# Six local-attention layers: probabilities in blocks of 32 queries by 64 keys, and another order of work on all engines

## The reference, cut to what matters

```python
def local_attention(q, k, v):
    b, h, n, d = q.shape            # 8, 16 heads, 512 tokens, 64
    w = WINDOW                      # 32
    ...
    bk2, bv2 = (look(bk), look(bv)) # each window of 32 with the one before it
    ...
    mask = (it < jb) | (it > jb + w) | (jb == -1)
    sim = jnp.einsum('bhwie,bhwje->bhwij', bq, bk2) * QK_SCALE
    sim = jnp.where(mask, -jnp.finfo(sim.dtype).max, sim)
    attn = jax.nn.softmax(sim, -1)
    out = jnp.einsum('bhwij,bhwje->bhwie', attn, bv2)
    return out.reshape(b, h, n, d)
```

## Time and profile before

| what | value |
|---|---|
| three runs | 3644.83, 3644.83, 3644.84 us (median 3644.83) |
| span of the profiled execution, first to last instruction | 3639.9 us |
| PE busy | 3554.4 us (98%), 47348 matmul instructions |
| PE weight loads busy | 3028.6 us (83%) |
| ACT busy | 3359.9 us (92%) |
| DVE busy | 3128.2 us (86%) |
| POOL busy | 2732.9 us (75%) |
| granted TensorE clock | 1.000 over the span |

### The profile page before, as it was taken

The page is one execution under the profiler, slowest core; times in us unless marked ns, Lnnn a source line. Parts: engine busy times, 40 slices in busy tenths (PEclk is TensorE's granted clock), DMA queues, the critical chain, the costliest instruction groups (busy, mean ns, idle before and its releaser), DMA issues.

```text
span 3639.9 us, 133048 instructions
## 1 busy us (share of the span) xinstructions
PE 3554.4 (98%) x47348; PEld 3028.6 (83%) x47348; DVE 3128.2 (86%) x7021; ACT 3359.9 (92%) x10928; POOL 2732.9 (75%) x2058
## 2 busy tenths in 40 slices
PE   8999999999999999999999999999999999999998
PEld 5666678888888888888888888888888888888887
DVE  8999988888888788887888888889888888888887
ACT  8999889999999999999999999999999999999996
POOL 0111288888888788788888888888888888888884
PEclk9999999999999999999999999999999999999999
DMA  2000011111111111111111111111111111111111
GB/s 102 7 14 10 14 38 43 35 32 34 44 43 41 28 36 36 39 46 36 33 33 40 40 45 35 33 30 43 47 35 37 30 33 45 34 35 36 42 36 39
DMA packets 165015, 132.71 MB, mean 36 GB/s; under 512 B 113933, under 2 KB 124813, under 8 KB 164109
## 3 DMA queue, kind: packets, MB, share of 16 engines
q1 hardware_dynamic: 164365, 124.19, 13.9%
HBM read 25.84 MB, written 4.19 MB: 8 GB/s over the span
## 4 chain that ended last, share of the span: by engine, by line
PE 75%; ACT 5%; DVE 4%; issue 3%; POOL 1%; ACTq 0%; POOLq 0%; DVEq 0%
PE bank L1103 10%; PE bank L1057 10%; PE bank L1082 8%; PE bank L1143 8%; PE bank L1125 6%; PE bank L1019 4%; PE bank L1020 4%; PE bank L1021 4%; PE bank L980 4%; PE bank L1118 3%; PE bank L953 2%; ACT late L1441 2%; PE bank L955 2%; PE bank L954 2%; PE bank L1033 2%
## 5 line engine op out<-in xcount | busy, mean ns | idle before, releaser
L1554 POOL TENSOR_TENSOR a_rn<-a_ssqc,a_minus_half 128x16 f32<-128x16 f32 x384 | 1113.2, 2899 | 490.3 <-DVE a_ssqc L1765 480.6
L1441 ACT ACTIVATE late<-bank,a_negmax 128x96 f32<-128x96 f32 x3072 | 1013.5, 363 | 11.8 <-DVE a_negmax L1714 10.7
L1577 POOL TENSOR_TENSOR a_r<-a_u,a_rn 128x512 f32<-128x512 f32 x768 | 788.3, 1046 | 0.6
L1564 POOL TENSOR_TENSOR a_PN<-late,a_erec 128x384 f32<-128x384 f32 x768 | 730.6, 971 | 9.1 <-PE bank L1082 8.2
L1441 ACT ACTIVATION_READ_ACCUMULATOR late<-bank,a_negmax 128x1 f32 x3072 | 708.7, 231 | 0.0
L1424 ACT ACTIVATE a_QK<-bank 128x512 f32<-128x512 f32 x768 | 467.8, 609 | 122.5 <-PE bank L1057 122.5
L1737 DVE TENSOR_TENSOR a_v<-bank,a_rot_s 128x512 f32<-128x512 f32 x768 | 523.1, 681 | 0.0
L1727 DVE TENSOR_TENSOR a_u<-bank,a_rot_c 128x512 f32<-128x512 f32 x768 | 521.4, 679 | 1.2 <-ACT a_sq L1417 1.1
L1417 ACT ACTIVATE a_sq<-bank 128x512 f32<-128x512 f32 x768 | 482.7, 628 | 42.2 <-PE bank L1021 12.9
L1402 ACT ACTIVATE late<-bank 128x512 f32<-128x512 f32 x758 | 479.6, 633 | 15.3 <-PE bank L1082 11.4
L1745 DVE TENSOR_TENSOR a_u<-a_u,a_v 128x1024 f32<-128x1024 f32 x384 | 489.5, 1275 | 0.7 <-issue 0.3
(11 more groups left out here) (191 smaller groups left out, 8129.7 us busy)
## 6 DMA issues: line engine op xcount, KB each, us to landing
a_V_even<-a_V_odd SPq DMA_DIRECT2D x384, 128.0 KB, 2.3
a_V_even<-a_V_odd SPq DMA_DIRECT2D x192, 64.0 KB, 2.2
late<-in_qkv SPq DMA_DIRECT2D x20, 384.0 KB, 3.8
a_x_sh<-X SPq DMA_DIRECT2D x48, 128.0 KB
a_V_even<-a_V_odd SPq DMA_DIRECT2D x192, 32.0 KB, 1.9
a_x_sh<-X SPq DMA_DIRECT2D x48, 127.0 KB
late<-X SPq DMA_DIRECT2D x47, 128.0 KB
late<-X SPq DMA_DIRECT2D x47, 127.0 KB
```

The source lines that it names most:

```text
L1441: ins = act.activation(E[:, s.par, k, :], scores[:, i % 2, col:col + KW], ACT.Exp, bias=negmax[:, s.par, k:k + 1], accum_out=esum[:, s.par ...
L1554: pool.tensor_tensor(rn[:, a.par, :], ssqc[:, a.par, :], minus_half[:, :], ALU.pow).then_inc(S["rn"], 1)
L1564: pool.tensor_tensor(PN[:, s.par, 2 * hp:2 * hp + 2, :].rearrange("p i (b k) -> p i b k", b=2)[:, :, :, 0:KW], spread(E[:, s.par, half, :] ...
L1577: pool.tensor_tensor(heads(r[:, a.par, half]), heads(u[:, a.par, half]), rn[:, a.par, mm * 2 * HG:(mm + 1) * 2 * HG].unsqueeze(2).to_broad ...
```

## The change

The block becomes 32 queries by 64 keys (KW = 2 * WIN). The scores of a pair are 8 x 64 columns on 128 partitions: the query windows c = 0 to 3 lie on partitions 32c to 32c + 31, head e in score bank e. PE's logits become 32 matmuls of 64 rows, 32 output partitions and 64 columns; its mask becomes 8 matmuls of 256 columns; the transposes of the probabilities become one set of four 128x128; the outputs become 32 matmuls of 64 rows, 64 output partitions and 32 columns, which write two banks (5 and 6), one for each half of the key partitions. ACT copies the transposed probabilities once, not twice, and the outputs from both banks in one instruction. The values are moved by DMA into V_sh, by 32 partitions, 96 rows and 32 rows in place of 64 and 32. The LAG constants and the order on PE, ACT, DVE and POOL change: on PE it becomes outputs, projections, values, then mask and logits, transposes of the probabilities, transposes of queries and keys 1, output projection, transposes of queries and keys 0. The norms, the second cosines and sines, the sum, and the power move one cycle later. The core of the diff (in the cycles of PE, ACT and DVE "..." stands for the lines taken out, which are in the kernel above):

```diff
-KW = 3 * WIN
+KW = 2 * WIN
...
-LAG_T, LAG_S, LAG_PT, LAG_O, LAG_Y = 2, 4, 6, 7, 7
+LAG_R, LAG_T0, LAG_T1, LAG_Q0, LAG_Q1, LAG_L, LAG_S, LAG_PT, LAG_O, LAG_Y = 1, 1, 2, 2, 3, 4, 5, 6, 7, 7
...
-    sb("masks", [P, 2, 2 * KW], BF16)
+    sb("masks", [P, 2, 4 * KW], BF16)
...
-    A["PT"] = view("layers", 16 * P, "p (s n q) -> p s n q", s=2, n=8)
-    A["OT"] = view("layers", 4 * CQ, "p (s e t) -> p s e t", s=2, e=2)
+    A["PT"] = view("layers", 16 * P)[:, 0:8 * P].rearrange("p (s n q) -> p s n q", s=2, n=4)
+    A["OT"] = view("layers", 4 * CQ, "p (s u h t) -> p s u h t", s=2, u=4, h=2)
...
-    sb("PN", [P, 2, 4, 2 * P])
+    sb("PN", [P, 2, 4, P])
...
-    p_qk, p_vo, p_ta, p_tb, p_y = banks[0:2], banks[2], banks[5], banks[6], banks[7]
+    p_qk, p_ta, p_vo, p_tb, p_y = banks[0:2], banks[2], banks[5], banks[6], banks[7]
+    p_o, p_both = (p_vo, p_tb), psum[:, 5:7, 0:CQ]
...
-                sp.dma_start(V_even[WIN:KW, a.g, m:m + 2, :], V_odd[0:64, a.g, m:m + 2, :]).then_inc(S[name], 16)
+                sp.dma_start(V_sh[WIN:P, a.g, m:m + 2, :], V_nat[0:P - WIN, a.g, m:m + 2, :]).then_inc(S[name], 16)
...
-                t = pair_at(n, p, LAG_T)
+                t = pair_at(n, p, LAG_T1 if mm else LAG_T0)
...
-                    ge(pe, S[f"pt_out{mm}"], done(n, p - (mm == 0), LAG_PT))
+                    if mm == 0:
+                        ge(pe, S["pt_out"], done(n, p, LAG_PT))
+                    else:
+                        ge(pe, S["o_out"], done(n, p, LAG_O))
...
-            def transpose_probs(n, p, hp):
...
-            def prob_transposes(t, hp):
-                for i in range(4):
-                    first = KW if i % 2 else 0
-                    ins = pe.transpose(p_t[hp][:, i * P:(i + 1) * P], PN[:, t.par, 2 * hp + i // 2, first:first + P], ident[:, :])
-                ins.then_inc(S[f"pt{hp}"], 1)
+                    for e in range(2):
+                        pe.wait_ge(S[f"pn{e}"], t.k + 1)
+                    pe.wait_ge(S["qk_out0"], done(n, p - 1, LAG_T0))
...
+            def prob_transposes(t):
+                for k in range(4):
+                    ins = pe.transpose(p_ta[:, k * P:(k + 1) * P], PN[:, t.par, k, :], ident[:, :])
+                ins.then_inc(S["pt"], 1)
...
+                    pe.wait_ge(S["qk_out1"], keys_out)
...
-                        for i in range(4):
-                            keys = slice(0, P if i % 2 else KW)
-                            V = (V_odd if i % 2 else V_even)[keys, o.g, 2 * o.half + i // 2, :]
-                            for e in range(2):
-                                q, c, side = slice(64 * e, 64 * e + 64), hp * P + 64 * e, 64 * ((e + i) % 2)
-                                ins = pe.matmul(p_vo[q, hp * CQ + i * 64:hp * CQ + (i + 1) * 64], V[:, c:c + DH],
-                                                PT[keys, o.par, 4 * hp + i, side:side + 64], start=True, stop=True)
+                        for c in range(4):
+                            m, own = divmod(c, 2)
+                            V, col = V_nat if own else V_sh, hp * P + c * WIN
+                            for half in range(2):
+                                keys = slice(KW * half, KW * half + KW)
+                                for e in range(2):
+                                    q, v = slice(64 * e, 64 * e + 64), hp * P + 64 * e
+                                    ins = pe.matmul(p_o[half][q, col:col + WIN], V[keys, o.g, 2 * o.half + m, v:v + DH],
+                                                    PT[keys, o.par, 2 * e + hp, c * WIN:(c + 1) * WIN], start=True, stop=True,
+                                                    skip_group_check=True)
                     ins.then_inc(S["o"], 1)
...
+                    for c in range(4):
+                        for e in range(2):
+                            rows = slice(WIN * c, WIN * c + WIN)
+                            pe.matmul(scores[rows, e, :], ident_b[sides[e], 64 * e:64 * e + WIN],
+                                      masks[sides[e], int(s.half > 0 or c > 0), :], start=True, stop=True, skip_group_check=True)
                     for hp in range(2):
-                        for i in range(2):
-                            for e in range(2):
-                                q = sides[e]
-                                pe.matmul(scores[sides[(e + i) % 2], i, hp * 2 * KW:(hp + 1) * 2 * KW], ident_b[q, q],
-                                          masks[q, int(s.half > 0 or i > 0), :], start=(hp == 0), stop=True, skip_group_check=True)
-                    for hp in range(2):
-                        for i in range(4):
-                            first, col = 64 * (4 * s.half + i), (2 * hp + i // 2) * KW
-                            for e in range(2):
-                                q = sides[e]
-                                ins = pe.matmul(scores[sides[(e + i) % 2], i % 2, col:col + KW],
-                                                QK[q, s.gpar, hp, WIN + first:WIN + first + 64],
-                                                QK[q, s.gpar, 2 + hp, first:first + KW], start=False, stop=True,
-                                                skip_group_check=True)
+                        for half in range(2):
+                            col = (2 * hp + half) * KW
+                            for c in range(4):
+                                first = (2 * s.half + c // 2) * P + half * KW + c % 2 * WIN
+                                for e in range(2):
+                                    ins = pe.matmul(scores[WIN * c:WIN * c + WIN, e, col:col + KW],
+                                                    QK[sides[e], s.gpar, hp, WIN + first:WIN + first + WIN],
+                                                    QK[sides[e], s.gpar, 2 + hp, first:first + KW], start=False, stop=True,
+                                                    skip_group_check=True)
                     ins.then_inc(S["logits"], 1)
...
             def cycle(n, p):
...
+                s = pair_at(n, p, LAG_L)
                 late_end(n, p)
+                outputs(pair_at(n, p, LAG_O), n * NP + p, done(n, p - 1, LAG_T1))
                 project(n, p, 0)
...
+                if p == P_GATE:
+                    up(n, p, 0, 0, p_ta)
+                if p == P_X:
+                    up(n, p, 2, 1, p_ta)
+                if p == P_VALUES:
+                    up(n, p, 0, 1, p_ta)
+                if p == P_TURN:
+                    turn(n)
+                project(n, p, 1)
+                if p == P_GATES:
+                    up(n, p, 1, 0, p_ta)
+                values(n, p)
+                late_pieces(n, p)
+                if p == P_BIAS:
+                    shifts(n)
+                if p == P_X and n + 1 < NI:
+                    transpose_x(n + 1)
+                if p == P_VALUES:
+                    up(n, p, 1, 1, p_tb)
+                if p == P_GATES:
+                    up(n, p, 2, 0, p_tb)
+                if p == P_GELU:
+                    down(n)
                 if s:
                     ge(pe, S["exp1"], s.k)
                 logits(s, p_s)
...
+                transpose_probs(n, p)
                 transpose_qk(n, p, 1)
                 output_projection(pair_at(n, p, LAG_Y))
...
+                transpose_qk(n, p, 0)
...
+            def probs(t):
                 if t:
...
+                    act.wait_ge(S["pt"], t.k + 1)
                     ge(act, S["o"], t.k - 1)
...
+                    act.activation(PT[:, t.par, :, :], p_ta.rearrange("p (n q) -> p n q", n=4), ACT.Copy).then_inc(S["pt_out"], 1)
 
             def outputs(o):
                 if o:
                     act.wait_ge(S["o"], o.k + 1)
                     ge(act, S["y"], o.k - 1)
...
+                    act.activation(OT[:, o.par, :, :, :].rearrange("p u h t -> p h u t"), p_both.rearrange("p h (u t) -> p h u t", u=4),
                                    ACT.Copy).then_inc(S["o_out"], 1)
...
             def cycle(n, p):
...
+                s = pair_at(n, p, LAG_S)
                 if n == 0 and 1 <= p <= 4:
                     late_outputs(2 * p - 2)
                     late_outputs(2 * p - 1)
...
+                queries_and_keys(pair_at(n, p, LAG_Q1), 1)
+                exps(s, 0, 0, p_s)
+                exps(s, 0, 1, p_s)
+                queries_and_keys(pair_at(n, p, LAG_Q0), 0)
+                exps(s, 1, 0, p_s)
+                outputs(pair_at(n, p, LAG_O))
+                exps(s, 1, 1, p_s)
+                if p == P_TURN:
+                    turned(n)
                 squares(n, p, 0)
...
+                if p == P_GATES:
+                    gate_out(n, 1, p_ta)
+                if p == P_GELU:
+                    gelu(n)
                 if p == P_GATE:
...
+                    gate_out(n, 0, p_ta)
+                squares(n, p, 1)
+                if p == P_GATES:
+                    gate_out(n, 2, p_tb)
                 if p == P_X and n + 1 < NI:
                     high_x(n + 1)
...
                 values(n, p)
```

(38 more changed lines are left out.)

304 lines of the change are left out of this document (103 added, 201 removed).

## The result

The changed kernel takes 3625.91 us, median of 4 runs (3620.24 to 3632.55), against 3644.84: ratio 0.9948, 95% interval 0.9936 to 0.996. It is faster by 19 us, half a per cent, where 241 us were forecast, and lies above the range of 3340 to 3600. The profiled execution took 3632.55 us with a span of 3630.7.

What follows compares the result with a forecast made beforehand. PE's work was taken as the bound. Its terms summed to -0.59 us a pair, -227 us over 384 pairs, and the new order gave -14 us, for a forecast of 3404 us; range 3340 to 3600 us.

Steps and rivals of the forecast that it cites:

- Transposes of the probabilities: On PE, two sets of four transposes become one, saving 0.44 us a pair; called the surest term.
- Logits: On PE, 64 small matmuls run eight at once in eight rounds, 0.44 us in all, saving 0.22 us a pair.
- rival of the issue: Issue sets PE's small matmuls at 0.0206 us each; the pair gains 0.53 us, the kernel slows to 3848 us; 13%.
- Mask: On PE, two rounds of 192 columns become one of 256, saving about 0.08 us a pair.
- Outputs: On PE, loading 64 stationary columns sets the round, so the outputs burst changes by 0 us a pair.
- Changes of shape: On PE, switches between small places and the whole array go from three to four, adding 0.15 us a pair.
- ACT, DVE, POOL: Their batch work falls to 57.4, about 53.4 and about 50.0 us; PE stays the bound, so worth nothing by itself.
- The new order: Across the engines' reordered steps, waits change by -0.3 us a batch, between -0.8 and +2; -14 us in all.
- A wait takes the gain: ACT comes too late for PE's values or outputs in most cycles, costing 115 us, time 3519 us; 14%.
- There is nothing to win or lose there: The granted clock already stands at 1.00, its upper level of 2.4 GHz, so no time can change there.
- The 4.9 us around the span: Time outside the profiled span, added to the forecast span of 3399 us to give 3404 us.
- the two marks: Signs of being wrong: small matmuls costing 0.0153 us or more each, or PE's idle time above 3 us a batch.

Runs made afterwards that it cites:

- a1: The changed kernel with the feed-forward statistics put last on DVE in cycle p = 0, not before the sum; 3537.75 us.
- a4: a1 with PE doing projection 1 before the first feed-forward matmul in cycle p = P_VALUES; 3531.79 us.
- a6: a4 with the squares of the first projection one place earlier on ACT, ahead of the exponentials; 3501.89 us.
- l2: a1 with half of the logits matmuls left out, 32 instructions a pair in place of 64; 3465.1 us, one run.
- o1: a1 with each outputs matmul streaming 16 columns of queries in place of 32; 3539.8 us, one run.
- o2: a6 with each outputs matmul loading 32 stationary columns in place of 64; 3444.8 us, one run.
- b1: The kernel before with the feed-forward statistics put forward on DVE, right behind the row maxima; 3789.2 us.
- a3: a1 with ACT's copy of queries and keys 0 ahead of the exponentials in the cycle behind the gelu; 3569.39 us.
- a5: a4 with the values ahead of projection 1 on PE in cycle p = 1; 3546.73 us.
- l1: a1 with each logits matmul streaming 32 columns of keys in place of 64; 3522.2 us, one run.

## Why the prediction was wrong

The sign, and PE as the bound, were right. Two steps failed: the rate at which small matmuls come, in the term of the logits, and the waits that the new order makes. The forecast batch was 60.3 us. The undisturbed batch is 3.8 us above it, 1.8 in PE's busy time (61.56 for 59.8) and 2.0 in its idle time (2.53 for 0.5). Over 48 batches that is 182 of the 222 us missed. The rest, 40 us, lies in the batches that ran disturbed, many of them with the clock at its lower level; this share is an account, not a test. The runs give a second account: the statistics are 88 us (a1), the late copy and the late squares together 36 (a4, a6), the logits 88 by their start times; that leaves 10 of the 222, and a6 lies 98 us above the forecast.

- **Transposes of the probabilities, -0.44.** Right: one set a pair is left, at 0.49 us up to the next start. Before, the two took 0.36 and 0.53.
- **Logits, -0.22.** The step that failed in the work. "If all eight run at once, it is eight rounds, 0.44 us": they do run at once, eight in 56 ns, for two rounds. Then the instructions don't come fast enough: 9.8 ns each over the burst (l2) and 8.3 at their steady rate, where 6.9 were needed. Measured +0.01, so 0.23 us a pair, 1.84 a batch, 88 us of the kernel. My rival of the issue had the mechanism, with the wrong size: I priced it at 0.0206 us an instruction, and it is 0.0098. That is under the 0.0153 us I had set as the deciding price, which was itself misplaced. At 0.0153 the 128 instructions cost 1.96 us, 0.44 above the 1.52 of the forecast, and the pair would still gain 0.15; by my own terms the gain ends at 0.0165 (1.52 + 0.59 over 128). I had bounded the price from above by the row and not thought of one between none and 0.0206. The row of before could not show it: there a round of four takes 83 ns, 21 an instruction, which the issue easily keeps up with. But the trace of before did show four starts within 10 ns, so 0.0206 us was never the price of an instruction.
- **Mask, -0.08.** Start to start from 0.189 to 0.120 us, -0.07.
- **Outputs, 0.** Right, and for the reason given: 1.083 to 1.065 us, with the stream ruled out (o1) and the stationary columns halved (o2).
- **Changes of shape, +0.15.** About right, as a remainder. The busy time of a batch falls by 0.37 us a pair, and a pair without feed-forward is 0.29 us shorter, start to start (6.92 to 6.63). With the terms above at -0.44, +0.01, -0.07 and -0.02, +0.15 to +0.23 are left for the shapes and everything else. One such step by itself: the last pass of the values, up to the next start, takes 0.21 us ahead of the mask and took 0.12 ahead of the transposes.
- **ACT, DVE, POOL.** Right: they shrank and none became the bound by its work.
- **The new order, -0.3 us a batch.** The step that failed in the waits, and the larger one. I weighed PE against ACT's three copies and DVE's addition. I didn't go through DVE's own list for what was moved past what: the statistics went ahead of the sum, and their DMA had been hidden by the very operations they were moved past. That is 1.3 us a batch (a1), 88 us in all with its after-effects. The undisturbed batch's idle time rose by 1.7 us where I took -0.3 and bounded it at +2. ACT late for PE was forecast once a batch and came once, 0.55 us. The late squares, which PE feels through DVE's cosines and sines (0.68 us, and 0.85 in a1), I had not named. "A wait takes the gain" was thus the best of the rivals, through DVE and a DMA and not through ACT.
- **"There is nothing to win or lose there" of the clock.** Wrong in one direction: with PE's stops, b1 and the kernel after lose it at times.
- **The 4.9 us around the span.** In the profiled run of the kernel after it is 1.9 us, a difference of 3 us.

Of the two marks I had set, idle time came near its own (2.5 us against 3) and the price of a small matmul stayed below (0.0098 against 0.0153). Both steps failed under their marks. The logits and the statistics together, 176 us, would put the time at 3580, still inside the range; the late copy and the late squares took it out.

What stays open: the clock's share of the 88 us of a1, beyond the estimate of 28, and why three batches of every eight, at the same places of each layer, take 1.4 us longer even in a6 (63.4 for 62.0), as some do in the kernel before (up to 66.6 for 65.3).

## What to carry to other kernels

When a hand-written order changes, go through every engine's list, not just the bounding one's, and for each step moved forward ask what it waits for and whether what it overtook was the cover; here one line of DVE was worth 88 us. When work is cut into more, smaller matmuls, price them twice, by columns and by instructions, and take the larger. Where a wait is moved along a strict order it tends to come up at the next place (a3, a5); follow it back to the engine that first had idle time it could not afford, and move that (a6).

## What the runs showed of the hardware

- fp32 matmuls with their loads in eight different places of the array start 3 to 4 ns apart, and the next eight start 56 ns behind the first with 64 columns and 28 ns with 32; but a long burst goes on at 8.3 ns each (the kernel after, l1 and o2), 9.8 ns over all 64. The Trainium skill, TensorE: Matmul & The Clock Gate, in its section on the 56 ns, gives about 25 ns as the least from start to start; the measurement decides: 8.3 ns sustained, for matmuls in different places.
- The fast part of a burst ends at a count of instructions. 8 mask matmuls and the first 24 logits are, with their loads, 64 instructions, and the 25th comes at 187 ns with 64 or 32 columns; in o2, with no mask ahead, the rounds of 32 ns last for 32 matmuls, again 64 with their loads. The Trainium skill, TensorE: Matmul & The Clock Gate (Back-to-back issue gap), speaks of a window of 64 instructions. The trace agrees with that.
- Short matmuls keep the rhythm of their stationary operand: 64 stationary columns in fp32 make rounds of 58 ns whether 32 or 16 columns stream (o1), and 32 stationary columns, which here write half the output partitions too, make rounds of 32 ns (o2).
- Stops of PE cost more than themselves. Between 600 and 3400 us of the span, every fall of the granted clock to its lower level (1.2 GHz) comes behind a stop of 1.25 to 2.4 us, in the kernel after and in b1. Over the whole span that level takes 119 us in the kernel after, 97 in b1 and 27 in a1, where one line of DVE is moved. By the estimate above each of these microseconds costs 0.3 us.
